# Two full-size identity matmuls ahead of each attention score product

## The reference

```
h = modulate(layernorm(x)); q, k, v = split(h @ w_qkv + b_qkv)
attn = softmax(q @ k.T * 9 ** -0.5);  x = x + gate * ((attn @ v) @ w_proj + b_proj)
x = x + gate * mlp(modulate(layernorm(x)))
```

## Time and profile before

| what | value |
| --- | --- |
| median of three runs | 1165.92 us |
| span of the profiled execution, first to last instruction | 1173.7 us (the page gives no other time for it) |
| TensorE busy | 948.9 us, 81% |
| VectorE busy | 713.6 us, 61% |
| ScalarE busy | 412.4 us, 35% |
| GpSimd busy | 198.5 us, 17% |
| chain that ended last | TensorE 61%, VectorE 29%, ScalarE 4%, issue 4% |
| mean granted TensorE clock | 0.638 |

### The profile page before, as it was taken

One profiled execution on the slowest core, in us unless ns is written; L12 is line 12 of the kernel. 1 busy time (PEld: TensorE's weight loads), 2 busy tenths in 40 slices (PEclk: granted clock), 3 DMA queues, 4 the chain that ended last, 5 costly groups with the idle time before them and its releaser, 6 DMA issues.

```text
span 1173.7 us, 12067 instructions
## 1 busy us (share of the span) xinstructions
PE 948.9 (81%) x3791; PEld 513.7 (44%) x3791; DVE 713.6 (61%) x2140; ACT 412.4 (35%) x742; POOL 198.5 (17%) x350
## 2 busy tenths in 40 slices
PE   4666889877898768889877788778887978989847
PEld 1432443335765433357644434535433534335326
DVE  4388767775353887772457767656677365564333
ACT  0302342324341333343424432415332436435412
POOL 5201014010240110042420000311002211012020
PEclk9999755556775655566866555657555656558556
DMA  3000001010111000001110000100000100000000
GB/s 101 13 1 10 16 6 43 1 29 1 29 29 29 17 1 1 1 16 42 34 38 0 1 1 1 29 1 1 1 1 0 30 0 1 1 1 1 6 5 11
DMA packets 22025, 16.01 MB, mean 14 GB/s; under 512 B 6427, under 2 KB 19391, under 8 KB 21962
## 3 DMA queue, kind: packets, MB, share of 16 engines
q1 hardware_dynamic: 21914, 15.22, 4.8%
q10 hardware_dynamic: 48, 0.02, 0.0%
HBM read 14.62 MB, written 0.61 MB: 13 GB/s over the span
## 4 chain that ended last, share of the span: by engine, by line
PE 61%; DVE 29%; issue 4%; ACT 4%; POOL 2%; DMA 0%; DVEq 0%; SPq 0%; ACTq 0%; POOLq 0%
PE o_bank L1289 11%; PE m_bank L1268 11%; DVE row_max L823 7%; PE s_bank L1257 3%; PE m_bank L1466 3%; PE d_bank L1350 3%; PE d_bank L1407 2%; PE d_bank L1409 2%; PE d_bank L1408 2%; PE m_bank L1276 2%; PE d_bank L1306 2%; PE d_bank L1307 2%; PE d_bank L1239 2%; PE d_bank L1392 2%; PE d_bank L1321 2%
## 5 line engine op out<-in xcount | busy, mean ns | idle before, releaser
L663 ACT ACTIVATE probs<-s_bank 128x512 f32<-128x512 f32 x384 | 220.4, 596 | 546.6 <-PE s_bank L1257 544.0
L823 DVE TENSOR_REDUCE row_max<-m_bank 128x1 fp32r<-128x512 f32 x384 | 256.0, 686 | 151.9 <-PE m_bank L1268 147.1
L1268 PE MATMUL m_bank<-k_t,q_t 32*128 32x512 f32 x384 | 216.5, 752 | 61.9 <-DVE q_rows L1079 24.2
L1257 PE MATMUL s_bank<-q_t,k_t 32*128 32x512 f32 x384 | 239.4, 749 | 5.8 <-ACT probs L663 4.9
L1289 PE MATMUL o_bank<-probs,v_aug 128*32 128x512 f32 x768 | 178.2, 1019 | 3.9 <-DVE o_tok L841 3.2
L1268 PEld LDWEIGHTS m_bank<-k_t,q_t 32*128 32x128 f32 x384 | 81.6, 271 | 181.9 <-issue 62.9
L1257 PEld LDWEIGHTS s_bank<-q_t,k_t 32*128 32x128 f32 x384 | 90.6, 272 | 30.9 <-ACT probs L663 16.1
L589 POOL TENSOR_TENSOR h_tok<-h_tok,mod 128x144 f32<-128x144 f32 x48 | 24.0, 499 | 297.3 <-DVE h_tok L882 297.3
L1407 PE MATMUL d_bank<-ff_hi,g_hi 128*128 128x144 f32 x192 | 60.7, 316 | 1.5 <-ACT g_hi L733 1.4
L1409 PE MATMUL d_bank<-ff_lo,g_hi 128*128 128x144 f32 x192 | 60.7, 316 | 0.0
L1408 PE MATMUL d_bank<-ff_hi,g_lo 128*128 128x144 f32 x192 | 60.5, 315 | 0.0
(11 more groups left out here) (232 smaller groups left out, 1639.4 us busy)
## 6 DMA issues: line engine op xcount, KB each, us to landing
raw_a<-in_L_cond_w_dram SPq DMA_DIRECT2D x20, 288.0 KB
raw_a<-in_L_cond_W_fc_dram SPq DMA_DIRECT2D x4, 288.0 KB
w_rows<-in_L_cond_W_dram SPq DMA_DIRECT2D x8, 141.8 KB
raw_d<-in_L_cond_w_dram SPq DMA_DIRECT2D x30, 36.0 KB
raw_a<-in_L_cond_w_dram SPq DMA_DIRECT2D x20, 36.0 KB
x_tok<-in_x_dram SPq DMA_DIRECT2D x2, 288.0 KB, 4.2
out_dram<-moe SPq DMA_DIRECT2D x4, 144.0 KB, 1.9
raw_d<-in_L_cond_w_dram SPq DMA_DIRECT2D x30, 4.0 KB
```

What stands on the lines that cost most here:

```text
L663: act.activation(probs[:, n % PROBS, :], s_banks[n % S_BANKS][:, :], ACT.Exp, scale=HD ** -0.5)\
L823: dve.tensor_reduce(row_max[:, grp % 2, t, MAXROW + 32 * j:MAXROW + 32 * j + 1], bk[:, :], AX.X, ALU.max).then_inc(drained, 1)
L1257: pe.matmul(s_banks[n % S_BANKS][:, :], k_t[rows, par, g, kt * P:(kt + 1) * P], q_t[rows, par, g, :], start=True, stop=True).then_inc(s["s ...
L1268: pe.matmul(bk[:, :], q_t[rows, par, g, t * P:(t + 1) * P], k_t[rows, par, g, :], start=True, stop=True).then_inc(s["max_full"], 1)
```

## The change

In `scores(n)`, after the waits and before the score product, two matmuls are issued: the 128x128 identity `ident_r` as weights, all 128 rows and 512 columns of `q_t` of this group as the moving operand, into the same `s_bank`. The score product that follows starts a new sum in that bank and overwrites them. No wait is added and no result depends on them.

```
+WARM = 2
...
                 if n >= S_BANKS:
                     pe.wait_ge(s["probs_ready"], n - S_BANKS + 1)
+                for _ in range(WARM):
+                    pe.matmul(s_banks[n % S_BANKS][:, :], ident_r[:, :], q_t[:, par, g, :], start=True, stop=True)
                 pe.matmul(s_banks[n % S_BANKS][:, :], k_t[rows, par, g, kt * P:(kt + 1) * P], q_t[rows, par, g, :],
                           start=True, stop=True).then_inc(s["scores_full"], 1)
```

## The result

The changed kernel takes 1491.29 us (median of four runs, 1480.39 to 1530.76), the kernel before 1164.53: a ratio of 1.278, 95% interval 1.271 to 1.285. Forecast were 1500 us, a ratio of 1.287, with a range of 1280 to 1630. The profiled execution has a span of 1487.8 us, 314.1 more than before.

A forecast was written before the change was run, and what follows sets the result against it. TensorE, mostly at its lower clock, bounds the kernel. 288 steps x 1.17 = 337 us, 54 x 0.5 = 27, less 30 from side work, on 1173.7 give 1508 us of span, 1500 us measured; range 1280 to 1630.

The forecast's parts named there:

- The max product loses its cover: On TensorE in each step, the max product no longer runs beside the score product and takes its own 0.72 us.
- 0.43 and 0.23 us for the first added matmul: Time from first to second added matmul on TensorE: 0.43 us at the lower clock, 0.23 us at the higher.
- 0.60 us from the second added matmul to the score: Second added matmul to score product: 0.60 us at the lower clock, bounded by 0.43 and 0.72; 0.33 at the higher.
- the 144-column row: Profile row nearest to the second added matmul's switch: followers after 0.21 us, 32-row follower after 0.35, a switch of 0.14.
- Ten steps without waits, 31.1 us: Ten pure attention steps at 0.50 need 31.1 us without any wait, against 19.36 before: 1.17 us a step more.
- The old waits go: In the attention loop, TensorE's old waits of 0.43 us a step, mostly for VectorE, are all given back.
- 30 from side work: The loop idles 33 us more than the piece's rate through side work; about 30 us of them come back.
- A quarter of the steps at 1.00: 96 of 384 loop steps run at the higher clock, costing about nothing against a step at 0.50 before.
- The rival with the higher clock in the whole loop: The added pair lifts the whole loop to the higher clock: about 1085 us, up to no change; chance 0.10.
- half the loop at the higher clock: Rival: 192 steps of the loop at the higher clock, 1370 us, down to 1280 with more; chance 0.17.
- the waits that stay: Rival: the loop's old waits are not given back, 1.6 us more in 288 steps, 1670 us; chance 0.08.
- the step that was at 1.00 already: A loop step already at the higher clock costs 0.5 us more: 0.43 + 0.56 added, 0.43 of wait back.

## Why the prediction was right, step by step

1. *The max product loses its cover, 0.72 us.* Right (856.11 to 856.83). Putting the pair ahead of the max product gave back 183 us, but most of that came with the clock: at 0.50 in both it is 0.30 of 1.23 us a step.
2. *0.43 and 0.23 us for the first added matmul.* Right: one matmul less shortened the way to the score by 0.42 us at 0.50.
3. *0.60 us from the second added matmul to the score.* Mis-sized: 0.72 at 0.50, the upper bound, and 0.44 instead of 0.33 at 1.00. Leaving a full-size product of 512 columns costs what leaving a 32-row one does; the 144-column row that I went by was no model for it.
4. *Ten steps without waits, 31.1 us.* They took 32.30 [window 872.60 to 904.90], at 0.50, with TensorE busy throughout; 0.12 us in ten steps explains 1.2 of the missing 1.2. The same holds beyond the piece: on 186 steps at 0.50 the price is 1.30 us, against 1.17 + 0.12.
5. *The old waits go.* Right in kind, too large in the sum: the loop idled 155 us before and 37 after, 118 us back. I had counted 0.43 us in 288 steps, 124, in 54 more, 23, and 30 from side work: 177 us, more than the loop had.
6. *A quarter of the steps at 1.00, at no cost against 0.50 before.* The share was 38%, 51 steps more than counted, worth some 60 us (51 x 1.17). The price was near: against a step at 0.50 before, -0.02 us in 23 steps of steps 0 to 287 and 0.14 in 75 of the last 96. What was too low is the price against a step that had stood at 1.00 already: 0.81 us in 15 of the last 96 and 1.00 in 7 others, not 0.5. The dearer switch (0.12 us in 237 steps, 28 us) and these steps work against the 60 us, so that the total came within 9 us is partly luck.
7. *The rival with the higher clock in the whole loop*, not slower at 1085 us up to no change, was wrong in its price, not only in its chance: the kernel with four matmuls had 87% of its steps at 1.00 and took 1426 us (without the two further ones, at 0.43 us a step as between the two kernels at 1.00, an estimated 1260), and the part of the changed kernel that was at 1.00 throughout was slower than before. Three of my sums are also off, and nothing rests on them: half the loop at the higher clock comes to 1378 us and not 1370, the waits that stay to 1680 and not 1670, and the step that was at 1.00 already to 0.56 and not 0.5.

Busy time as the profile counts it did not lift the clock: the ten steps stand at 0.50 with 32.30 of 32.30 us busy. The sentence of the Trainium skill that I weighed ("TensorE: Matmul & The Clock Gate", section "Why this matters for your kernels") does not hold here if that busy time is taken for it.

What stays open: why the last blocks hold 1.00 with two matmuls and steps 0 to 287 do not. With one matmul and with two of 64 columns the last 96 steps stood at 0.59 and 0.53, with two and four of full length at 1.00; with the pair ahead of the max product 128 of steps 0 to 287 stood at 1.00, by their score products, instead of 50. No run separates the waits from the side work, and the same pair on the same last 96 steps stood at 0.83 when the first four blocks had no added matmuls.

## What to carry to other kernels

Before adding work to an in-order engine, look at what its neighbours do together: here the added matmuls cost less by their streaming (0.23 to 0.50 us a step at 0.50) than by their full-size shape (0.61 to 0.88). A part of that is a concurrency of 32-row products that it ends, which no busy figure shows, only equal start times in the timeline. A higher granted clock is worth what the stage's own products gain from it; in the last 96 steps here that was less than the pair and its switches. And compare steps at the same clock: from the totals alone, all of the 183 us seemed to be the order of the matmuls. Dose such a change, too: one, two and four matmuls took 1504, 1491 and 1426 us, which no single dose would have told.

## What the runs showed of the hardware that was not expected

- Four added matmuls a step made the kernel faster than two, 1426 against 1491 us, as 87 instead of 38% of the steps ran at 1.00. One took 1504 us, with 8%; its interval and that of two meet at 1.285.
- Leaving a shape costs the same 0.29 us over the streaming (0.72 for 512 columns at 0.50) from 32 to 128 rows and from 128 to 32; at 1.00 it is about 0.2.
- Two full-size matmuls of 64 columns ahead of a 32-row product take 0.56 us, half of the 1.15 of two with 512; on the same 32 rows 0.45.
